# Layers 0 and 1 of a four-layer kernel: composed offset matrices, keys and values turned in 32x32 blocks on VectorE, two background jobs a slot, attention projection one tile later

## What is computed

```python
mask = jax.nn.sigmoid(conv1x1(pconv(q_img, pconv_mask_w), w_mask, b_mask))
for i in range(G):
    off = conv1x1(pconv(q_img, pconv_off_w[i]), w_off[i], b_off[i])
    dil = 2 * i + 1
    k_list.append(deform_sample(kv[0, :, i], off, mask, dil, dil * PAD))
    v_list.append(deform_sample(kv[1, :, i], off, mask, dil, dil * PAD))
attn = jax.nn.softmax(jnp.einsum('bgnc,bgckn->bgnk', qf, ks_), axis=-1)
out = jnp.einsum('bgnk,bgckn->bgnc', attn, vs_)
return out @ w_proj + b_proj
```

## Time and profile before

| | us |
|---|---|
| median of 3 runs | 9839.31 |
| lowest, highest | 9834.57, 9847.19 |
| the profiled execution: device time | 9855.23 |
| its span in the trace | 9853.4 |
| in it: ahead of the first gather | 217.3 |
| in it: first to last gather | 6752.0 |
| PE, DVE, ACT, POOL busy over the span | 3062.5, 5717.2, 1524.3, 4639.8 |

### The profile page before, as it was taken

How to read it: one execution, slowest core, us unless ns; L and a number is a source line. 1 busy time by engine, 2 the same in 40 slices (tenths; PEclk the granted TensorE clock), 3 DMA queues, 4 the chain that set the end, 5 groups by cost and what they waited for, 6 DMA issues and landing times. The chain is left out here.

```text
span 9853.4 us, 106326 instructions
## 1 busy us (share of the span) xinstructions
PE 3062.5 (31%) x41476; PEld 2212.3 (22%) x41476; DVE 5717.2 (58%) x6511; ACT 1524.3 (15%) x3478; POOL 4639.8 (47%) x4747
## 2 busy tenths in 40 slices
PE   3102101021001001021001100111245476899997
PEld 2000000000001000010000000000224365788885
DVE  6486574765754456765754455544574465555554
ACT  1000000000000000000000000100122132444442
POOL 0776677665777557766777566765200000000000
PEclk7556555555555555555555555555577788999998
DMA  4433345332453224333453234332221532222224
GB/s 86 121 107 98 88 115 145 105 93 85 117 147 99 83 83 124 102 103 90 114 150 99 80 89 117 102 91 74 52 44 71 162 93 82 71 67 64 67 67 176
DMA packets 822918, 966.47 MB, mean 98 GB/s; under 512 B 283029, under 2 KB 643561, under 8 KB 817897
## 3 DMA queue, kind: packets, MB, share of 16 engines
q0 software_dynamic: 221184, 604.27, 20.7%
q1 hardware_dynamic: 573880, 321.25, 13.3%
q10 hardware_dynamic: 27440, 34.87, 1.0%
HBM read 797.64 MB, written 155.99 MB: 97 GB/s over the span
## 5 line engine op out<-in xcount | busy, mean ns | idle before, releaser
L512 POOL DMA_INDIRECT l_rec<-records,l_row x4608 | 4583.7, 995 | 2384.4 <-issue 1423.6
L673 PE MATMUL l_pso<-l_id,l_att_t 128*128 128x128 f32 x128 | 60.8, 475 | 4714.6 <-DVE l_att_t L1074 2549.4
L1056 DVE TENSOR_TENSOR l_rec<-l_rec,l_psv 128x4608 f32<-128x4608 f32 x128 | 634.0, 4953 | 1044.7 <-DMA l_rec<-records,l_row 892.4
L673 PEld LDWEIGHTS l_pso<-l_id,l_att_t 128*128 128x128 f32 x128 | 23.3, 182 | 4781.9 <-DVE l_att_t L1074 2585.9
L1074 DVE TENSOR_REDUCE l_att_t<-l_rec 128x128 f32<-128x4608 f32 x128 | 1004.2, 7845 | 4.4
L2329 DVE COPY l3p_mix<-l3p_ps 128x512 f32<-128x512 f32 x1024 | 659.8, 686 | 576.6 <-PE l3p_ps L2205 576.6
L2291 ACT ACTIVATE l3p_mix<-l3p_ps 128x512 f32<-128x512 f32 x1024 | 556.7, 596 | 663.9 <-PE l3p_ps L2205 663.9
L1057 DVE TENSOR_REDUCE l_psv<-l_rec 128x144 f32<-128x4608 f32 x128 | 635.0, 4961 | 4.4
L1072 DVE TENSOR_TENSOR l_rec<-l_rec,l_psv 128x4608 f32<-128x4608 f32 x128 | 634.0, 4953 | 6.0 <-issue 1.6
L2205 PE MATMUL l3p_ps<-l3p_psi,l3p_ms 32*128 32x128 f32 x16384 | 612.4, 283 | 21.2 <-DVE l3p_mix L2329 16.6
L2166 POOL COPY l3p_four<-l3p_fil 128x128 f32 (+1 forms) x64 | 18.7, 293 | 1198.9 <-PE l3p_psm L2258 1197.8
(11 more groups left out here) (358 smaller groups left out, 6120.4 us busy)
## 6 DMA issues: line engine op xcount, KB each, us to landing
l_rec<-records,l_row POOLq DMA_INDIRECT x4608
l2b_w<-l_w SPq DMA_DIRECT2D x32, 1024.0 KB, 10.9
records<-l_area SPq DMA_DIRECT2D x48, 512.0 KB
l_row<-meta SPq DMA_DIRECT2D x124, 154.0 KB
l_x_hat<-l3a_xout ACTq DMA_DIRECT2D x32, 512.0 KB, 4.4
l3p_xin<-l_x_hat SPq DMA_DIRECT2D x128, 128.0 KB, 3.1
l_y_raw<-l3p_yr SPq DMA_DIRECT2D x64, 256.0 KB, 3.0
l3p_yin<-l_y_raw SPq DMA_DIRECT2D x128, 128.0 KB, 2.9
```

The source lines that it names most:

```text
L512: pool.indirect_dma_start(out=rec[:, r, c % HT, :], out_offset=None, in_=records[b].rearrange("r c d -> r (c d)"), in_offset=bass.Indirect ...
L1056: step(dve.tensor_tensor(keys, keys, asked.broadcast_to([P, GROUPS, TAPS * CORNERS, HC]), ALU.mult))
```

## The change

1. **Offsets with composed matrices.** Since nothing stands between the 3x3 convolution and the 1x1 convolution, the two matrices are multiplied once, ahead of the loop (slot 8 of `points(0)`, six small matmuls and one ACT copy into `we_s`). A job `offc` is then three matmuls with `we_s` on the shifted copies and one with `wc_s`, and `off4`, `offm`, their ACT copies and `conv4` as their buffer go. The first image uses the same path.
2. **Keys and values in blocks.** The jobs `kt` and `vt` go. DVE turns k and v itself, one instruction of 128x4096 for each (`blocks_of`), as 32x32 blocks. `keep` reads the new layout: 32 partitions and 64 rows of an image for each group, where it read 64 partitions and 32 rows. `a_chan` moves to the buffer of k.
3. **At most two jobs a slot** in `points` (`qkv` from six, `qt`, `off4`, `offm` from three, `offs` from four), over more slots; ACT empties a job two slots, that is one tile, later, in `points` and in `linear`. Where slots are full, `qt` and the first `offc` share one.
4. **Filters of v** now stand in slots 30 to 33 and 39 to 42, filters of q one slot earlier; the transposes in slots 43 and 44. `points` has 46 slots in place of 47, `linear` 39 in place of 38, so the sum over the loop is 255 as before. In `linear` the steps behind its products and behind `o` stand one or two slots later.
5. **Attention a tile later.** ACT's copy `turned`, PE's projection and DVE's `add` run one tile later; `add(t)` waits for PE's transpose of tile t+1.
6. `pconv` weights are loaded once, not for each image.

```diff
-        opening = [("qkv", (f, g), 5 + f) for f in range(3) for g in range(NG)]
...
-        beside = [("qkv", (f, g), 5 + (NG * f + g) // 6) for f in range(3) for g in range(NG)]
-        beside += [("qt", g, 18 + g // 3) for g in range(NG)]
-        beside += [("off4", g, 21 + g // 3) for g in range(NG)] + [("offm", g, 21 + (NG + g) // 3) for g in range(NG)]
-        beside += [("offc", g, 28 + g // 4) for g in range(NG)] + [("offs", g, 30 + g // 4) for g in range(NG)]
-        beside += sorted([("kt", g, 39 + g // 2) for g in range(NG)] + [("vt", g, 38 + g) for g in range(NG)], key=lambda j: j[2])
...
+        beside = [("qkv", (f, g), 5 + (NG * f + g) // 2) for f in range(3) for g in range(NG)]
+        beside += sorted([("qt", g, 17 + g // 2) for g in range(NG)] + [("offc", g, 20 + g) for g in range(NG)], key=lambda j: j[2])
+        beside += [("offs", g, 28 + g // 2) for g in range(NG)]
...
-                            for dy in range(3):
-                                last = pe.matmul(bank[0:m, :], wp_s[:, dy, o:o + m], pads[0][0:3 * HC, 8 * at + dy:8 * at + dy + 8, 0:W],
-                                                 start=dy == 0, stop=dy == 2)
...
+                                pe.matmul(o, we_s[:, dy, :], pads[0][0:3 * HC, 8 * at + dy:8 * at + dy + 8, 0:W], start=dy == 0, stop=False)
                             last = pe.matmul(o, wc_s[:, :], q_img[:, at * 512:at * 512 + 512], start=False, stop=True)
...
                 pe.wait_ge(s_dve, summed(t))
+                if t >= 1:
+                    project(t - 1)
                 pe.transpose(ps_a, att_t[t % 2][:, :], id_s[:, :]).then_inc(s_att, 1)
-                project(t)
...
-                        if own + int(b >= 1 and kind != "qkv") != slot or kind == "offs":
+                        if own + 2 * int(b >= 1) != slot or kind == "offs":
...
-                        if own + 1 != slot:
+                        if own + 2 != slot:
...
                 weigh(t)
+                if t >= 2:
+                    store(t - 2)
                 if t >= 1:
-                    store(t - 1)
-                turned(t)
+                    turned(t - 1)
...
+                def blocks_of(f):
+                    kept = kv_t if b else kv_t0
+                    dve.transpose(kept[:, :, f - 1, :], img[f].rearrange("p (j s) -> p j s", s=HC)).then_inc(a_blk, 1)
...
-                dve.wait_ge(s_proj, t + 1)
+                if t + 1 < TILES:
+                    dve.wait_ge(s_att, t + 2)
+                else:
+                    dve.wait_ge(s_proj, t + 1)
...
-                if t >= 1:
-                    add(t - 1, step)
...
+                if t >= 2:
+                    add(t - 2, step)
```

More of the change, by code:

```diff
@@ L536, in points @@
                 for slot in range(PG):
-                    if slot == 15 and b == 0:
+                    if slot == 8 and b == 0:
                         pe.wait_ge(s_const, CONSTS)
-                        pe.wait_ge(s_zero, 4)
+                        pe.wait_ge(s_zero, 5)
+                        for dy in range(3):
+                            o = effect[:, OFFS * dy:OFFS * dy + OFFS]
+                            pe.matmul(o, wt_s[:, dy, :], wa_s[:, :], start=True, stop=False)
+                            mm = pe.matmul(o, wt_m[:, dy, :], wm_s[:, :], start=False, stop=True)
+                        mm.then_inc(a_form, 1)
                     if slot == 3:
-                        pe.wait_ge(a_x, b * 80 + 80)
+                        pe.wait_ge(a_x, loaded(b))
                         pe.wait_ge(a_stat, b + 1)
@@ L571, in points @@
                             for t in range(4):
                                 i = 4 * at + t
-                                last = pe.transpose(bank[:, t * P:t * P + P], src[:, i * P:i * P + P], id_s[:, :])
-                        if kind in ("off4", "offm"):
+                                last = pe.transpose(bank[:, t * P:t * P + P], q_img[:, i * P:i * P + P], id_s[:, :])
+                        if kind == "offc":
                             if at == 0:
                                 pe.wait_ge(a_shift, b * 48 + 64)
-                            m, o = (P, 0) if kind == "off4" else (HC, P)
+                                pe.wait_ge(a_eff, 1)
+                            o = bank[0:OFFS, :]
@@ L590, in points @@
                                 last = pe.transpose(bank[:, t * P:t * P + OFFS], conv4[0:OFFS, i * P:i * P + P], id_s[0:OFFS, 0:OFFS])
-                        if kind == "offs" and not b:
-                            pe.wait_ge(a_act, done_act + taken(pj, after(pj, "offm")))
-                            for t in range(4):
-                                i = 4 * at + t
-                                o = bank[:, t * P:t * P + OFFS]
-                                pe.matmul(o, conv4[:, i * P:i * P + P], wa_s[:, :], start=True, stop=False)
-                                last = pe.matmul(o, q_img[:, i * P:i * P + P], wc_s[:, :], start=False, stop=True)
                         last.then_inc(a_job, 1)
@@ L687, in points @@
                         act.activation(sc[:, 2:3], sc[:, 4:5], ACT.Sqrt).then_inc(a_std, 1)
+                    if slot == 8 and b == 0:
+                        act.wait_ge(a_form, 1)
+                        act.activation(we_s[:, :, :].rearrange("p d k -> p (d k)"), effect, ACT.Copy).then_inc(a_eff, 1)
                     if slot == 15 and b == 0:
@@ L1010, in linear @@
                         step_l(ins)
-                    if slot == 33:
+                    if slot == 35:
                         for t in range(NT):
@@ L1080, in _ @@
             step = Chain(dve, s_dve, s_gate[2], begun(TILES))
-            add(TILES - 1, step)
-            assert step.base + step.n == added(TILES - 1)
+            for t in (TILES - 2, TILES - 1):
+                add(t, step)
+                assert step.base + step.n == added(t)
             whole(linear(BATCH - 1))
```

205 lines of the change are left out of this document (103 added, 102 removed).

## The result

| | before | changed |
|---|---|---|
| median (us) | 9841.13 (4 runs, 9834.57 to 9847.19) | 9598.24 (4 runs, 9597.36 to 9602.01) |
| span of the profiled execution | 9853.4 | 9596.8 |
| first gather | 217.3 | 209.4 |
| first to last gather | 6752.0 | 6533.4 |
| end of the last gather to the end | 2884.1 | 2854.0 |

The ratio is 0.9754, 95% interval 0.9737 to 0.9771: **243 us or 2.5% faster**. Of the 256.6 us between the two spans 7.9 lie ahead of the loop, 218.6 in it and 30.1 behind it.

A forecast was written before the change was run, and what follows sets the result against it. No compute engine was full; gathers sustain 1.40 us each, and POOL stops when DVE, waiting for late PE results, frees buffers late. Terms −123 + 2 + 0 − 21 = −142 gave 9839.3 − 142 = 9697 us, range 9440 to 9800.

The forecast's parts named there:

- rival B: In the linears, a tile of slack takes stops below the backlog: up to 205 us more, 9492, half 9595; chance 0.22.
- `points`, −123: In points, fewer MATMUL rows and later copies remove all POOL stops: 123 us gained, bounds 60 and 123.
- The start, +2: Before the first gather, two DVE turns add 2 us, bounds 0 and +8; keep's price taken as unchanged.
- The linears, 0: In the linears, 304 rows an image unchanged, PE stays late: 0 gained of 205 us, bounds 0 and −205.
- the backlog of 27: In the gather loop, a POOL stop costs only what exceeds the backlog, put at 27.4 us from the fill.
- a tile that PE did long before: At DVE's add, the wait for PE's transpose was put at nothing, as that tile's was done long before.
- The end, −21: Behind the last gather, lag falls from 39 to 10 us, wide passes add 8: −21, bounds −30 and 0.
- C: In points, slow gathers come from PE's side traffic, so fewer rows run nearer 1.25 us: about 9450; chance 0.09.
- D: In the linears, a turn's fifth and sixth jobs wait for ACT, PE idles: 528 us slower, 10,225; chance 0.09.
- E: In the loop, points' stops go but a full backlog at each linear gives back over 120 us: about 9830; chance 0.08.
- The rule that PE and ACT never wait on anyone: A Trainium skill rule making PE no problem; the prediction said the trace disagrees, 15.4 us a job against 2.7.

The follow-up runs named there:

- Experiment 7: Changed kernel with offc rows as before in points(1), ACT copies one slot after PE in points(2) and linear(0), split products in linear(1): 9668.1 us first pace, 8875.7 second.
- experiment 2: Changed kernel with ACT emptying jobs one slot after PE's slot instead of two: 8872.7 and 8874.7 us, ratios 0.9997 and 1.0003 to the kernel before, second pace.

## Why the prediction came out as it did

The forecast was 9697 us and the range 9440 to 9800; measured were 9598. The sign and the mechanism in `points` were right, the linears' term was not: the forecast had 142 of the 243 us, and the range holds the result because it reached over rival B.

- **`points`, −123: measured −123.** No stop is left in the first 55 tiles. At tile 12, where ACT's copies of a job came 15.4 to 16.8 us apart, the two `offc` jobs of eight rows cost ACT one wait of 17.1 us, ahead of the second copy, and the next exponential is on time. What was tried of it is the rows: with the old number of rows, and everything else as changed, POOL stops again and `points(1)` loses 31.8 us. The two stretches of the earlier trace rows behind the fill, which hold it and the start of `points(2)`, had lost 30. So the number of rows is enough to bring a loss of this size back. That the fewer rows (composed matrices, turns on DVE) are most of the gain fits this and is not shown apart from their spread, as the repeated rows stand closer than the old ones. The two jobs a slot and the later offsets were not tried alone.
- **The start, +2: measured −8.** The turn cost what was taken: 4.43 us for 128x4096 in the groups view, the pace of a plain pass (4.41). That agrees with the Trainium skill, "Vector Engine (DVE) Microarchitecture Reference", § 3.8 The reshape front-end and per-opcode configuration, which has a 32x32 transpose sustain one element per cycle per lane. But `keep` was put at an unchanged price. It begins 1.4 us later, and its sixteen issues take 42.1 us from 32 partitions where they took 50.0 from 64:

```profile
L860 DVE STREAM_TRANSPOSE l_area<-l_area 128x4096 f32<-128x4096 f32 x6 | 26.5, 4431 | 0.3 <-DVE l_area L847 0.3
160.33 42.10 SPq L426 DMA_DIRECT2D records<-l_rec  x16
```

- **The linears, 0: measured −96 (205 to 110).** This is the step that failed: "a wait of 77 less 25 to 50 is still at or over the backlog of 27. I take 0". The bound was right and the value was not. Each linear has several waits, only one of which is 77 us, and the slack shortened all of them, that one too (L994 has 36.7 us at worst). The three longest stops of POOL in `linear(0)` were 37, 46 and 30 us and are 23, 21 and 37. Experiment 7 shows the cause for `linear(0)`: 34 us of 61 hang on ACT's copies. If the other two linears gained as much, which was not tried, it would be 103, against 96. The longest wait for another engine is now 56.3 us, at `add`, which no step of the prediction named as late, since it was set down as "a tile that PE did long before":

```profile
3444.32 0.29 DVE L1046 TENSOR_TENSOR l_done<-l_pso,l_res 128x128 f32<-128x128 f32 x1 [56.32 <-remote]
```

- **The end, −21: measured −30, of which −18 are the change's.** The lag of the last tile's first step fell from 39.0 to 7.6 us (10 was taken), and the two wide passes stand on the path as said:

```profile
6741.87 0.95 POOL L520 DMA_INDIRECT l_rec<-records,l_row  x1 [0.30 <-issue]
6750.38 4.95 DVE L1065 TENSOR_TENSOR l_rec<-l_rec,l_psv 128x4608 f32<-128x4608 f32 x1
6776.11 4.41 DVE L1033 TENSOR_TENSOR l_area<-l_area,l_pss 128x4096 f32<-128x4096 f32 x1
6785.23 0.29 DVE L1046 TENSOR_TENSOR l_done<-l_pso,l_res 128x128 f32<-128x128 f32 x1 [0.26 <-DVE l_area L1034]
```

  From the last gather to DVE's last step of `linear(3)` it is 208.9 us before and 191.2 now, 17.7 less. The other 12.4 lie in layers 2 and 3, whose code is the same: 2676.1 us behind that step in the profiled execution before and 2663.7 now (2663 to 2671 in the twelve other traces). Lag and passes by themselves would give 31.4 less 8, 23 us; where the other 5 went was not traced.
- **The sum.** −123, −8, −96 and −18 are −245, against 243 between the medians. The profiled execution before was 14 us over its median, and the 12.4 us of the later layers are most of that.
- **Rival B** gave 9595 for half of the linears' loss, and that is what happened: 96 of 205. Its case for it, stops each under one tile, is what the trace shows; that the time itself agrees to 3 us is luck, as the start's 10 us make up for the 7 that the linears gave less and the 3 of the end. **C** is refuted: with two fifths fewer rows in `points` a gather still takes 1.40 us (720 in 1008.2, 1008 in 1411.3). **D** did not come: the stops of the linears fell. **E** did not either: `linear(2)`, which starts on a full backlog, has the same stops as `linear(0)`.
- **The rule that PE and ACT never wait on anyone** (the Trainium skill, "SBUF — State Buffer", § Who interferes with whom) would have made PE no problem. Rows every 2.80 us with 0.26 us of work in each show PE held up at the first pace. By what, the trace does not say; that it is a port is not shown either. At the second pace the rule fits. PE is not alone: DVE's short steps around the last gather (start, us; the changed kernel) come 1.40 us apart at the first pace, and all 32 of them run through at the second (the first run of experiment 2):

```profile
6738.84 0.34 DVE L1028 TENSOR_SCALAR l_area<-l_area 128x128 f32<-128x128 f32 x1 [0.98 <-issue]
6740.23 0.34 DVE L1028 TENSOR_SCALAR l_area<-l_area 128x128 f32<-128x128 f32 x1 [1.05 <-issue]
```

```profile
6007.01 8.56 DVE L1028 TENSOR_SCALAR l_area<-l_area 128x128 f32<-128x128 f32 x32
```

  So the hold is on instructions of more than one engine, with nothing named that they wait for.

What stays open: why there are two paces, and what holds PE and DVE at the first. The first gathers cost the same at both. Here are the DMA queues from 300 to 430 us, at the first pace (the changed kernel again) and at the second (experiment 7's kernel; packets, MB, share of 16 engines; then issues, and us to landing where there is one):

```profile
q0 software_dynamic: 4985, 13.61, 35.0%
l_rec<-records,l_row POOLq DMA_INDIRECT x105
```

```profile
q0 software_dynamic: 4993, 13.65, 35.5%
l_rec<-records,l_row POOLq DMA_INDIRECT x105, 2.7
```

A packet takes the same time at both, 0.146 and 0.148 us, and from 1700 to 1900 us, where gathers come at 1.40 and 1.25 us, it still does (6864 packets in 31.9% and 7752 in 36.3%, 0.149 and 0.150 us). So the DMA engines are no slower. The first pace's traces have no landing time for the gathers, nor for the other DMAs of the loop; what that means is not known. Also open: the kernel before has no trace at the second pace, so it is not known where it makes up for the later start and end that it has at the first.

## What to carry to other kernels

Where engines run beside a long run of gathers from GpSimd, count instructions, not work: 2.80 us a MATMUL row set what was late here, and with the old number of rows a stage lost 31.8 us again. Give each result a round of slack before it is waited for, and read the loss as what exceeds the backlog, since a stop lets everything behind it catch up; so an over-full stage costs its stops, not its sum. When one wait is the longest, look at what would be waited for next: `add` hides an exponential that is as late. Time such a change on more than one occasion, beside the kernel before each time: this one is worth 243 us at one pace. At the other the changed kernel itself did not run, but five edited forms of it stand within 0.12% of the kernel before, and the sixth, with split products, is 0.21% slower.

## What the runs showed of the hardware

- Two paces of the same program: gathers at 1.25 us throughout and PE never late (8872 us for the kernel before), or 1.40 us once some 230 us (184 gathers) have passed without a stop (9841 us). The edited kernels are level with the kernel before at one, and the changed kernel is 243 us faster at the other. Number 3 stands as the chip of a run at each.
- While gathers run at the first pace, issued 1.25 or 1.40 us apart, rows that pile up are taken every 2.80 us (now and then 2.10) whether a row works 0.26 or 1.01 us, at a granted clock of 0.50 and 0.51; in the tile shown the first 26 are handed on at full speed (5.65 us), and some 17 to 27 us after POOL stops all go at full speed again. Short DVE steps come 1.40 us apart in the same way.
- The same 16 DMAs were issued in 42.1 us from 32 partitions with 64 rows each, and in 50.0 from 64 partitions with 32.
